# A transformer stack of eight layers on one core: ternary products in bfloat16, first loads and steps rearranged, one bank moved, a new order

## What is computed

```python
x = x + L0_xattn(ln(x), ctx, pos, pos)      # 32 heads of 8, axial rope on q and k
x = x + L0_ffn(ln(x))                        # product keys, 4 x 8 of 2048 experts
x = x + L1_xattn(ln(x), ctx, mask)           # 16 query heads of 128, 8 key heads
x = x + L1_ffn(ln(x))                        # 7 routed experts, top 2, and a shared one
x = x + L2_xattn(ln(x), ctx)                 # 16 heads of 16, two context parts
x = x + L2_ffn(ln(x))                        # ternary weights, see below
x = x + L3_xattn(ln(x), ctx)                 # 16 heads of 128, rms norm on q and k
x = x + L3_ffn(ln(x))                        # values quantised in blocks of 32
```

```python
def ternary_quant(w):
    s = jnp.mean(jnp.abs(w))
    q = jnp.clip(jnp.round(w / s), -1.0, 1.0) * s      # -s, 0 or s
h1 = x @ ternary_quant(w1).T                           # 256 -> 682
h3 = x @ ternary_quant(w3).T
out = (silu(h1) * h3) @ ternary_quant(w2).T            # 682 -> 256
```

## Time and profile before

| | |
|---|---|
| median of 3 runs | 2403.78 us (2400.72 to 2405.5) |
| the profiled execution | 2401.38 us |
| its span, first to last instruction | 2399.6 us |
| TensorE busy | 2246.8 us, 94% |
| VectorE busy | 1726.7 us, 72% |
| ScalarE busy | 1191.1 us, 50% |
| GpSimd busy | 442.1 us, 18% |
| TensorE in the chain that ended last | 67% of the span, VectorE 19%, ScalarE 7% |

### The profile page before, as it was taken

The page is one execution under the profiler, slowest core; times in us unless marked ns, Lnnn a source line. Parts: engine busy times, 40 slices in busy tenths (PEclk is TensorE's granted clock), DMA queues, the critical chain, the costliest instruction groups (busy, mean ns, idle before and its releaser), DMA issues.

```text
span 2399.6 us, 43628 instructions
## 1 busy us (share of the span) xinstructions
PE 2246.8 (94%) x16070; PEld 1770.9 (74%) x16070; DVE 1726.7 (72%) x4676; ACT 1191.1 (50%) x3095; POOL 442.1 (18%) x514
## 2 busy tenths in 40 slices
PE   4899999999999999988989999999999999998987
PEld 3666999999988888877977878885666666654554
DVE  5997977788567676665466886327677767779997
ACT  2677877777645444435623434114555555553111
POOL 2221100000001111011166550002222222220000
PEclk8999999999999999998998999999999999999999
DMA  9200300000110000012211100121000000000000
GB/s 338 79 2 2 111 1 2 1 2 1 57 55 14 10 10 14 10 36 82 78 45 32 45 1 1 47 77 53 1 1 1 1 1 1 1 1 1 14 11 12
DMA packets 53403, 75.12 MB, mean 31 GB/s; under 512 B 4966, under 2 KB 45944, under 8 KB 52168
## 3 DMA queue, kind: packets, MB, share of 16 engines
q1 hardware_dynamic: 48296, 58.96, 7.4%
q0 software_dynamic: 4896, 13.38, 1.7%
HBM read 45.58 MB, written 26.74 MB: 30 GB/s over the span
## 4 chain that ended last, share of the span: by engine, by line
PE 67%; DVE 19%; ACT 7%; issue 4%; POOL 1%; another core or an unknown queue 0%; DMA 0%; SPq 0%; DVEq 0%; ACTq 0%; POOLq 0%
PE pb L968 5%; PE pb L976 5%; PE pb L982 5%; PE pb L889 4%; PE pb L1147 4%; PE pb L1038 4%; PE pb L1010 3%; ACT workA L1513 3%; PE pb L915 2%; PE pb L1018 2%; PE pb L1155 2%; PE pb L1030 2%; PE pb L1210 2%; PE pb L1218 2%; PE pb L1087 1%
## 5 line engine op out<-in xcount | busy, mean ns | idle before, releaser
L2267 POOL TENSOR_TENSOR sm<-sm,neghalf 128x1 f32<-128x1 f32 x128 | 72.2, 564 | 1088.8 <-DVE sm L1591 1088.6
L1381 ACT ACTIVATE areaB<-i128h,workB 128x128 f16<-128x128 f16 x512 | 156.4, 393 | 31.7 <-DVE workB L1816 31.4
L1513 ACT ACTIVATE workA<-pb,workA 128x128 f32<-128x128 f32 x256 | 113.9, 457 | 78.4 <-DVE workA L2136 78.3
L1338 ACT ACTIVATE areaA<-pb 128x512 f32<-128x512 f32 x192 | 106.0, 601 | 59.3 <-PE pb L889 59.1
L1408 ACT ACTIVATE workA<-workA 128x128 f32<-128x128 f32 x256 | 99.4, 390 | 64.3 <-DVE workA L1853 64.3
L1218 PE MATMUL pb<-areaA,workA 128*128 128x256 f32 x512 | 122.8, 383 | 8.2 <-DVE workA L2148 8.2
L889 PE MATMUL pb<-workA 32*128 32x128 f16 (+2 forms) x2048 | 119.4, 255 | 10.7 <-DVE workA L1701 4.4
L1010 PE MATMUL pb<-xT,areaA 128*128 128x128 f32 x1024 | 124.6, 276 | 0.0
L968 PE MATMUL pb<-areaB 128*128 128x128 f32 x1024 | 124.2, 277 | 0.0
L889 PEld LDWEIGHTS pb<-workA 32*128 32x128 f16 (+2 forms) x2048 | 90.6, 143 | 44.2 <-issue 26.3
L1010 PEld LDWEIGHTS pb<-xT,areaA 128*128 128x128 f32 x1024 | 120.2, 192 | 3.4 <-issue 2.9
(11 more groups left out here) (406 smaller groups left out, 5804.4 us busy)
## 6 DMA issues: line engine op xcount, KB each, us to landing
rows_in<-areaB SPq DMA_DIRECT2D x7, 2048.0 KB, 16.7
areaA<-rows_in SPq DMA_DIRECT2D x38, 128.0 KB, 2.0
rows_out<-areaA POOLq DMA_DIRECT2D x38, 128.0 KB, 2.0
areaA<-in_L_xattn_Wo SPq DMA_DIRECT2D x2, 2048.0 KB, 15.6
areaB<-in_edT SPq DMA_DIRECT2D x1, 2048.0 KB, 9.9
areaB<-in_L_ffn_e_up SPq DMA_DIRECT2D x1, 2048.0 KB, 15.3
areaA<-in_wq1T SPq DMA_DIRECT2D x1, 2048.0 KB, 8.2
areaA<-in_L_xattn_Wq SPq DMA_DIRECT2D x1, 2048.0 KB, 8.1
```

What stands on the lines that cost most here:

```text
L1338: eng.activation(u.P[n % RP], bank(s, tag, b, c // 2)[:, :], ACT.Exp, scale=1.0 / math.sqrt(hd)).then_inc(freed(s, tag, b, c // 2)[0], 1)
L1381: m = eng.activation(u.far[:, g], i128h[:, :], ACT.Square, bias=u.at[b % 2][:, 1, 8 * c + g:8 * c + g + 1])
L1513: m = eng.activation(u.P[i][:, h], p[:, h * 128:(h + 1) * 128], ACT.Exp, accum_out=u.den[i][:, h:h + 1], bias=u.nb[i][:, h:h + 1], scale=u ...
```

## The change

1. **Ternary products.** The weights are stored as bfloat16 signs (-1, 0 or 1; two instructions for a chunk instead of four). x's transpose and the hidden values g are split into three bfloat16 parts that add up to them exactly: ScalarE casts the first part, VectorE subtracts it, copies the rest as second part and subtracts again for the third (steps `sp` and `gs`, function `split`). Each float32 product becomes three bfloat16 products into the same bank. The scales are applied at silu, at the multiply and at the add into x.
2. **Start.** The context is loaded in two pieces, blocks 0 and 1 ahead of the stage's weights and the rest after x's second part. The seven small loads are issued after the weights of stage 1. The angles become a step `tg` in the lists of VectorE and ScalarE; `mkey` and `gp` are made in step `mb` of stage 2. GpSimd's `pow` waits for `half_done`, its constant.
3. **Bank.** The output product of stage 7 goes to bank 0 instead of bank 7.
4. **Order.** All four strings are new. VectorE's begins lnA 0, tg, lnB 0, lnA 1, lnB 1, rope 0 and TensorE's xT 0, qk 0, xT 1, vp 0, vp 1, qk 1. In the middle of stage 5 TensorE's runs h(b,0), xT, h(b,1), out(b-1), h(b+1,0), h(b+1,1), xT, out(b), and VectorE's h(b,0), sp(b+1), gs(b,0), out(b-1), h(b,1), lnB, h(b+1,0), gs(b,1), gs(b+1,0). In TensorE's, the outputs of blocks 0 to 10 of stage 7 stand between the last `wo` of block 14 and that of block 15 of stage 6. After the last `wo` of block 14, VectorE's list before has 15 lnA, 15 lnB, 15 qa, 32 gu, 16 qh and 16 out of stage 7, the new one 12, 12, 12, 31, 16 and 16, and both the same steps of stage 6.

```diff
-    5: (("lnA", 1, "VG"), ("lnB", 1, "V"), ("xT", 1, "TA"), ("h", 2, "TAV"), ("out", 1, "TV")),
+    5: (("lnA", 1, "VG"), ("lnB", 1, "V"), ("xT", 1, "TA"), ("sp", 1, "AV"), ("h", 2, "TAV"), ("gs", 2, "AV"), ("out", 1, "TV")),
...
-    0: (("init", 1, "G"),),
+    0: (("init", 1, "G"), ("tg", 1, "VA")),
...
-    (7, "out"): lambda b, c: (("out", 7),),
+    (7, "out"): lambda b, c: (("out", 0),),
...
+        def ctx_here(b):
+
+            return (S["ctx_a"] if b < 2 else S["ctx_b"], 16)
+
...
         def xT_idle(s, b):
-            return full(s, last_xT[s][0], b, last_xT[s][1])
+            return full(s, last_xT[s][0], b, last_xT[s][1]) if s != 5 else (S["t_xs"], b + 1)
...
+            eng.dma_start(ctxT[:, 0:256], A["ctxT"][:, 0:256]).then_inc(S["ctx_a"], 16)
             weights(FIRST)
-            eng.dma_start(ctxT[:, :], A["ctxT"]).then_inc(S["ctx_in"], 16)
             for j in range(1, 4):
                 lo, hi = x_part[j]
                 eng.dma_start(x[:, lo:hi], xs[:, lo:hi]).then_inc(x_in[j], 16)
-            eng.dma_start(m8[:, :], A["maskT"]).then_inc(S["small_in"], 16)
...
+                if j == 1:
+                    eng.dma_start(ctxT[:, 256:], A["ctxT"][:, 256:]).then_inc(S["ctx_b"], 16)
+
+            def small():
+                eng.dma_start(m8[:, :], A["maskT"]).then_inc(S["small_in"], 16)
...
                 if k == 1:
+                    small()
                     zeros()
...
-                    t.wait_ge(*freed(5, "xT", b))
+                    t.wait_ge(S["t_xs"], b + 1)
...
                             for k in range(2):
-                                m = eng.matmul(p[0:M, m_ * 128:(m_ + 1) * 128], wm[:, k, mt * 128:mt * 128 + M], xT[:, k, :],
-                                               start=(k == 0), stop=(k == 1))
+                                for q in range(3):
+                                    m = eng.matmul(p[0:M, m_ * 128:(m_ + 1) * 128], wm[:, k, mt * 128:mt * 128 + M], u.xs[b % 2][:, q, k],
+                                                   start=(k + q == 0), stop=(k + q == 3))
...
                 elif step == "out":
-                    t.wait_ge(*freed(5, "h3", b, 1))
+                    t.wait_ge(S["t_gs"], nth(b, 1, 2))
...
-                        m = eng.matmul(p[:, 0:256], u.g[b % 2][0:M, k, :], w.w2[0:M, k, :], start=(k == 0), stop=(k == 5))
+                        for q in range(3):
+                            m = eng.matmul(p[:, 0:256], u.gs[b % 2][0:M, q, k], w.w2[0:M, k, :], start=(k + q == 0), stop=(k + q == 7))
...
+                if step == "sp":
+                    a.wait_ge(*freed(5, "xT", b))
+                    if b >= 2:
+                        a.wait_ge(*full(5, "h3", b - 2, 1))
+                    eng.copy(u.xs[b % 2][:, 0], ring_xT(5, b)).then_inc(S["t_hi"], 1)
+                elif step == "gs":
+                    a.wait_ge(*freed(5, "h3", b, c))
+                    if b >= 2:
+                        a.wait_ge(*full(5, "out", b - 2))
+                    eng.copy(u.gs[b % 2][:, 0, cols], u.g[b % 2][:, cols]).then_inc(S["t_ghi"], 1)
...
+                elif step == "tg":
+                    a.wait_ge(S["arg_done"], 1)
+                    eng.activation(cs[:, 1, :], arg[:, 0], ACT.Sin)
+                    eng.activation(cs[:, 0, :], arg[:, 1], ACT.Sin).then_inc(S["cs_done"], 1)
...
+            def split(ap, hi, mid, lo, done):
+
+                eng.tensor_tensor(ap, ap, hi, ALU.subtract).then_inc(*v.mark())
+                v.settle()
+                eng.tensor_copy(mid, ap).then_inc(*v.mark())
+                v.settle()
+                eng.tensor_tensor(lo, ap, mid, ALU.subtract).then_inc(done, 1)
...
                 if step == "mb":
+                    v.wait_ge(S["small_in"], small_all)
+                    eng.tensor_copy(mkey[:, :], m8[:, :]).then_inc(S["mkey_done"], 1)
+                    eng.tensor_tensor(gp[:, :], gqk[:, 0:1], gqk[:, 1:2], ALU.mult).then_inc(S["gp_done"], 1)
...
-                    eng.scalar_tensor_tensor(m, r, sm[0:rows, 12 + q:13 + q], m, ALU.is_lt, ALU.subtract).then_inc(*v.mark())
-                    v.settle()
-                    eng.scalar_tensor_tensor(m, m, sm[0:rows, 16 + q:17 + q], r, ALU.mult, ALU.subtract).then_inc(*v.mark())
-                    v.settle()
-                    eng.tensor_tensor(r, r, m, ALU.add).then_inc(S["t_q"], 1)
+                    eng.scalar_tensor_tensor(sign, r, sm[0:rows, 12 + q:13 + q], m, ALU.is_lt, ALU.subtract).then_inc(S["t_q"], 1)
...
-                        eng.tensor_tensor(g[:, 0:4, :].rearrange("p k n -> p (k n)"), u.a[0], p[:, :],
-                                          ALU.mult).then_inc(freed(5, "h3", b, c)[0], 1)
+                        eng.scalar_tensor_tensor(g[:, 0:4, :].rearrange("p k n -> p (k n)"), p[:, :], sm[:, 17:18], u.a[0],
+                                                 ALU.mult, ALU.mult).then_inc(freed(5, "h3", b, c)[0], 1)
...
-            v.wait_ge(S["small_in"], small_all)
-            eng.tensor_copy(mkey[:, :], m8[:, :]).then_inc(S["const_done"], 1)
-            eng.tensor_tensor(gp[:, :], gqk[:, 0:1], gqk[:, 1:2], ALU.mult).then_inc(S["gp_done"], 1)
-            v.wait_ge(S["const_done"], 1)
-            v.wait_ge(S["gp_done"], 1)
+            eng.memset(neghalf[:, :], -0.5).then_inc(S["half_done"], 1)
```

More of the change, by code:

```diff
@@ L562, in program @@
         u5.xT = [carve(256).rearrange("p (k n) -> p k n", k=2) for _ in range(3)]
+        u5.xs = [carve(384).bitcast(BF16).rearrange("p (q k n) -> p q k n", q=3, k=2) for _ in range(2)]
+        u5.gs = [carve(1152).bitcast(BF16).rearrange("p (q k n) -> p q k n", q=3, k=6) for _ in range(2)]
         w6, u6 = Bag(), Bag()
@@ L1132, in ternary @@
             def ternary(step, b, c):
[L1133 removed]
+                w, u = w5, u5
                 if step == "tp" and c == 1:
@@ L1467, in ternary @@
                 u = u5
-                if step == "h":
+                cols = slice(4, 6) if c else slice(0, 4)
+                if step == "sp":
[8 more added lines that the diff above has]
+                    eng.copy(u.gs[b % 2][:, 0, cols], u.g[b % 2][:, cols]).then_inc(S["t_ghi"], 1)
+                elif step == "h":
                     a.wait_ge(*full(5, "h1", b, c))
@@ L1474, in ternary @@
                     if c == 0:
-                        eng.activation(u.a[0], p[:, :], ACT.Silu).then_inc(freed(5, "h1", b, c)[0], 1)
+                        eng.activation(u.a[0], p[:, :], ACT.Silu, scale=u.sm[:, 16:17]).then_inc(freed(5, "h1", b, c)[0], 1)
                     else:
-                        eng.activation(u.a[1][:, 0:128], p[:, 0:128], ACT.Silu)
-                        eng.activation(u.a[1][0:42, 128:256], p[0:42, 128:256], ACT.Silu).then_inc(freed(5, "h1", b, c)[0], 1)
+                        eng.activation(u.a[1][:, 0:128], p[:, 0:128], ACT.Silu, scale=u.sm[:, 16:17])
+                        eng.activation(u.a[1][0:42, 128:256], p[0:42, 128:256], ACT.Silu,
+                                       scale=u.sm[0:42, 16:17]).then_inc(freed(5, "h1", b, c)[0], 1)
             def wide_heads(step, b, c):
@@ L1616, in centre, with angles @@
                 eng.tensor_tensor(g3, g3, bc(mu, 2, [128, n, 16]), ALU.subtract).then_inc(*v.mark())
+            def angles():
+                v.wait_ge(S["c_in"], c_all)
+                p3 = pos[:, :].rearrange("p (b q) -> p b q", q=2)
+                a4 = ang.rearrange("p (b q j) -> p b q j", q=2, j=2)
+                eng.tensor_copy(a4[:, :, :, 0], p3)
+                eng.tensor_scalar(a4[:, :, :, 1], p3, float(np.float32(0.01)), None, ALU.mult).then_inc(*v.mark())
+                v.settle()
+                MAGIC = 12582912.0
+                for k, off in ((0, 0.0), (1, math.pi / 2)):
+                    a0 = arg[:, k]
+                    eng.tensor_scalar(a0, ang, off, None, ALU.add).then_inc(*v.mark())
+                    v.settle()
+                    eng.tensor_scalar(turn, a0, 1.0 / (2 * math.pi), MAGIC, ALU.mult, ALU.add).then_inc(*v.mark())
+                    v.settle()
+                    eng.tensor_scalar(turn, turn, MAGIC, None, ALU.subtract).then_inc(*v.mark())
+                    v.settle()
+                    eng.scalar_tensor_tensor(a0, turn, -6.28125, a0, ALU.mult, ALU.add).then_inc(*v.mark())
+                    v.settle()
+                    eng.scalar_tensor_tensor(a0, turn, -(2 * math.pi - 6.28125), a0, ALU.mult, ALU.add).then_inc(*v.mark())
+                    v.settle()
+                    m = eng.tensor_scalar(a0, a0, 3.1415925, -3.1415925, ALU.min, ALU.max)
+                    m.then_inc(*(v.mark() if k == 0 else (S["arg_done"], 1)))
+                eng.tensor_copy(idh[:, :], ident)
+                eng.tensor_copy(i128h[:, :], cst[:, C_I128:C_I128 + 128]).then_inc(S["const_done"], 1)
             def small_heads(s, step, b, c):
@@ L2051, in ternary @@
                 chunk = ((0, 1364, 128), (1364, 2728, 128), (2728, 4008, 128), (4008, 4264, 42))
```

(7 more changed lines are left out.)

205 lines of the change are left out of this document (96 added, 109 removed).

## The result

Four runs of the changed kernel took 2383.6 to 2389.75 us, median **2387.34**; the kernel before, on the same chip, 2400.72 to 2405.8, median 2404.64. The ratio is 0.993 (95% interval 0.9911 to 0.9948). It gained 17 us, not the 36 of the forecast.

A forecast was written before the change was run, and what follows sets the result against it. TensorE, busy 2246.8 of 2399.6 us, was taken as the bound, with VectorE setting the tail. Savings 11.5 + 16 + 1.5 + 7 = 36 us gave 2365.4 for the profiled execution, median 2368 us; eight-in-ten range 2350 to 2389.

The forecast's parts named there:

- start: Kernel start: layer norm no longer waits for small loads, so the first rope comes earlier; 11.5 us saved, bounds 9 to 12.5.
- products: Stage 5: bfloat16 products replace float32 ones on TensorE; 22 us saved over 16 blocks.
- given back for VectorE's chain: Stage 5: outputs wait for added VectorE instructions, 0.5 to 1 us uncovered every second block; 6 of the 22 us lost.
- preparation of the weights: Inside stage 4: two of four VectorE instructions per chunk go, about 10 us less VectorE work; 1.5 us saved.
- tail: Stages 6 and 7: norms, quantisations and one multiply move from VectorE's tail into stage 6; 7 us saved.
- all other reordering: Remaining changes of the order lists, which the prediction could not price; 0, with 4 us either way.
- So the shift is carried: After the start: TensorE, 94% busy, does the same work from an earlier start, so the gain of 11.5 us lasts.
- Rivals B: Stage 5: load and product pairs cost 0.081 us, so the products gain nothing in sum; 2384 us, chance 0.06.
- C: Stage 5: loads not hidden at all, 1.5 us more a block than before; 2408 us, chance 0.04.
- Rival A: Stage 5: VectorE becomes the bound, exposed chain 2 us a block takes back the products' gain; 2384 us, chance 0.17.
- Bank 0: 0, at worst 5: Stages 6 and 7: sharing bank 0 with xT and stage 6's q costs nothing, at worst 5 us.
- Signs named ahead: Prediction would be wrong if the first rope came later than 17 us or stage 5's stretch took over 212 us.

The follow-up runs named there:

- start undone: Kernel after with the start of the kernel before (small loads and whole context ahead, angles and mkey in front); 0.9954 of the kernel before.
- start alone: Kernel before with only the change's new start, plus the new list for stage 0's first four blocks; 0.9954 of the kernel before, 11.0 us.
- two parts: Kernel after with each split computing only two bfloat16 parts, the third zero-filled but still multiplied; 0.9885 of the kernel before, beside 0.9895 for after.
- tail undone: Kernel after with the old order from the middle of stage 6 (block 7) on and stage 7's output in bank 7 again; 0.9938 of the kernel before.
- The one cut: Kernel after with the old order for the first half of stage 1 only, to the ninth block's gathers; 0.9892 of the kernel before.

## Why the prediction was wrong, point by point

| step | forecast | measured | from |
|---|---|---|---|
| start | 11.5 | 6.3 to 13.6, on average 9.1 (traces), 9.4 and 11.0 (medians) | thirteen traces; start undone, start alone |
| products | 22 | 34 | 6.62 against 8.76 us a block |
| given back for VectorE's chain | 6 | 7 | two parts |
| preparation of the weights | 1.5 | not measured by itself | TensorE idles 4.5 us less ahead of the products, with the new order |
| these three together | 17.5 | 23.5 | last combine to stage 6's first add |
| tail | 7 | 6.0 (traces), 5.5 (medians) | tail undone |
| all other reordering | 0, 4 either way | **-21** | 16.1 in stage 1, 4.6 in stage 0 and its hand-over |
| sum | 36 | 17 | 9.1 + 23.5 + 6.0 - 20.7 = 17.9 |

That the sum of the terms meets the 17 so closely is in part luck: they come from several executions, the start alone varies by 7 us between them, and over its three comparisons the kernel after won 20 us on average.

**The step that failed** is the sentence "the remaining reordering I cannot price: 0, with 4 either way". It was not a term without a price: the stage in question was the fullest of the kernel. Before, TensorE idled 2.2 of 408 us in stage 1, at a full clock; a new list with the same products could win at most those 2.2 us there, and lose any number. A zero with bounds alike on both sides was wrong in kind. The new list of stage 1 made TensorE idle 10.3 us more, mostly waiting for ScalarE and VectorE, and half clock behind the gaps cost 5.5 us more; another 4.6 us went in stage 0 and its hand-over. The three ternary terms, together 6 us too small, hid part of the miss.

**Start.** Layer norm at 3.45 (forecast near 3.6), transpose at 9.99 (10), rope at 14.43 (14.3): each as worked out. "So the shift is carried" was right from 70 us on; ahead of that 0 to 5 us go, depending on how long half clock lasts in the execution (14 to 27 us; 17 in the old profile, whose window 42 to 54 us was to be seen at 0.50). I had not asked what it would do. Why it is short in some executions of the same steps stays open.

**Products.** The mechanism was right and the term too small: the float16 transposes at 0.0625 us were near, the products took 0.056, the 0.42 us of the 42-wide ones is still there, and of the output's odd 0.38 some 0.2 are left. The bound that I worked out and did not take (0.0558 and 0.108 us, 32 us in all) was nearly right; the runs give 34. Rivals B and C are out with it. The Trainium skill (TensorE: Matmul & The Clock Gate, "Back-to-back issue gap") gives about 81 ns for such a pair; the trace has 56, so the measurement decides. By that rule h would have taken an estimated 6.25 us a block, more than the 5.78 before; it took 4.45.

**VectorE's chain.** 70.7 us more in stage 5 (114.7 in 142 us, before 44.0 in 155) against 73 forecast, a period of 15.5 us for two blocks where I had said near 8 each, a wait of 1.56 in every second block where I had said 0.5 to 1. Given back: 7, forecast 6. Rival A gave almost the measured time and is false: TensorE stayed the fuller engine (186.6 us busy against VectorE's 170.8, forecast 191 and 176). But the stretch took 205.9 us and not the 202 of the forecast: TensorE idles for 14 us more, and the half of it that is not the chain's, among it the gap of 4.2 us at the start of stage 6, I had not seen. **A total that fits a rival is no sign for the rival.**

**Tail.** 14 us less VectorE in the tail (12.6 measured), 4 us more TensorE in stage 6 (4.6), net 7 (6.0). "Bank 0: 0, at worst 5" held only beside the new order; beside the old one it was 79.

**Signs named ahead.** I wrote that the prediction would be wrong if stage 5's stretch took over 212 us; it took 205.9 (1478.34 to 1684.24). The rope was in time. Both signs said right, and the time still was wrong: I had named none for the stages 1 to 4, whose order changed as well.

What stays open: which steps of the new stage 1 list bring the gaps. The one cut at which both lists agree on all four engines made a wait of its own.

## What to carry to other kernels

Where a change rewrites an order written by hand, price it stage by stage with the idle time that TensorE has there before: a stage at 99% can hardly win and can lose, and the 10.6 us of new idle here brought 5.5 more by a lower clock. A bank, a shortened step and the order around them are one edit; undoing one of them alone (84 and 50 us here) measures the mismatch, not the part. Follow the lead at a few marked instructions through the whole trace before explaining a total, and through every trace that shares the program up to there: that tells which differences are the edit's (stage 1, the same within 1 us each time) and which are the execution's (the start, 7 us apart).

## What the hardware showed that I had not expected

The same instructions take different times in different executions, by the clock and by waiting. From the last tiles to the last combine the kernel after has

```profile
1225.00:1378.00 153.00, 139.09 (x1217) 116.52 (x1217) 109.84 (x308) 54.57 (x107) 104.28 (x77) 0.91 0.10 30
```

and the kernel with the old ternary stage, which has the same steps in the same order up to there, on another chip,

```profile
1225.00:1362.00 137.00, 130.95 (x1221) 109.95 (x1221) 110.51 (x309) 54.54 (x106) 104.41 (x77) 0.96 0.12 34
```

16 us between two executions. TensorE's busy time differs by 8 us, at a clock of 0.91 against 0.96, and its idle time by 8 (13.9 against 6.05). In this stretch all four traces of that chip idle for 6.0 us and all the others for 11.8 to 13.9, whatever the edit; why stays open. The 16 us are as much as the whole change brought, which is why an effect of 5 us was read here at marked instructions ahead of this place and not from medians. And on a TensorE that is otherwise full, gaps of 2.0 and 2.2 us were followed by stretches at 1.2 GHz: with the gaps filled by products that nobody reads, the stage was 5.5 us shorter.
